# Perceiver cross-attention block: one projection two steps earlier, one PSUM copy on another engine, one exponential ahead of a Gelu

## The chip, the cores and the metric

One core of a Trainium2 chip runs the whole program. Five engines work in parallel, each through its own list of instructions in order, and wait for each other by semaphores: TensorE (matmuls, PE in the profile, its weight loads PEld), VectorE (DVE), ScalarE (ACT), GpSimd (POOL), and SyncE (SP), which here only issues DMAs. The metric is the device time of one execution in microseconds, the median of several.

## The reference, cut to what matters

The block takes `x` (16 batches x 64 rows x 256) and a context (16 batches x 1601 rows x 256) and applies three sublayers with layer norms and residuals. Only the first one, the cross-attention, is touched:

```
Q, K, V = linear(norm(x)), linear(ctx), linear(ctx)      # 16 heads of 16
scores  = Q K^T / 4
feats   = mean(scores), mean of row maxima, variance of softmax(scores)   # per head
hidden  = gelu(linear(gelu(linear(feats))))              # exact gelu, width 64
t       = exp(clip(linear(hidden)))                      # one temperature per head
out     = softmax(Q K^T / (2 t)) V
```

So each batch needs two passes over the scores: a first one for the statistics, from which a small perceptron makes a temperature per head, and a second one with that temperature, whose exponentials are multiplied with V. The second sublayer is a gated state-space mixer, the third a feed-forward net with 4-bit block quantization; in the kernel they are the "tail" of each pair of batches.

## The kernel before, in words

**Slots and steps.** `run` goes through slots, one per batch `b` (from -1 to 19), each of 32 steps (`STEPS`). Every engine has its own `slot` function, which goes through the same 32 steps and issues what belongs to them; since each engine is in order, this written order is the schedule. In slot `b` three things overlap: the first pass of batch `b` (all 32 steps, one unit of scores each: `scores` on TensorE L651, maximum on VectorE L1179, exponential on ScalarE L909, `bn_stats` on VectorE L1185), the second pass of batch `b-1`, and the projections of the context. The tail of each pair of batches is spread over two slots and more.

**First pass.** Unit `u` is a chunk of 400 keys of a pair of heads. TensorE issues scores `u` and `u+1` in even steps. Three PSUM banks and three SBUF rings hold them, so scores `u` wait for exponential `u-3` (`before`). ScalarE runs exponential `u` in step `u+1` (`exp1`), VectorE the sums in step `u+2`.

**Second pass.** Unit `v` (0 to 27, two key tiles of a row group of heads each) has its scores in step `S2_AT[v]`: steps 14 to 37 and 40 to 43, where 32 and more are steps of the next slot; 38 and 39 (steps 6 and 7 of the next slot) are idle. Two units' scores go together (`scores2`, L667 and L677), ScalarE's exponential (`exp2`, L918) comes one step after its unit's, the multiplication with V (`values`, L694) two steps after the scores. So unit 22's exponential stands in step 5 and unit 23's in step 6, and both units' values in step 6. `exp2` writes one of five rings (`pring`), and waits for the multiplication that used the ring before.

**Projections.** `PJ_PLAN` says in which step TensorE projects a tile of 256 context rows into keys (`("k", tile, off)`, L605) or values (`("v", tile, off)`, L612); `off` 0 is this slot's batch, 1 the next one's. All go through one PSUM bank (`pjp`): a projection waits until the last one has been copied away (`pj_free`). ScalarE copies it one step later (`project`, L882 for keys, L869 for values), GpSimd adds up the keys for the mean two steps after the projection (`key_sums`, L1069). The context tile itself must have been split in two parts (`split_context` on ScalarE, L900, and a subtraction on GpSimd, L1083), in the steps of `CTX_AT`; the split of the next tile that uses the same buffer waits for the values' projection.

**Temperature.** `statistics` on VectorE runs in steps 1, 3, 8 and 10. TensorE's three small matmuls (`temperature`, L631, L634, L636) stand in steps 5, 6 and 7; in step 7, which is odd, the small matmul stands behind a projection if there is one. ScalarE's first Gelu is the last thing in step 5, its second the first in step 6 (`gelu`, L888). Gelu and Exp are in different tables, so there is a table load before the first Gelu and one before the exponential that follows. VectorE clips in step 8 (L1230, L1234), ScalarE turns the clipped value into the temperature first thing in step 9 (L985), ahead of that step's `exp2` and `exp1`; VectorE scales Q with it in step 10, and the `("m",)` entry in step 13 (L592) makes the row of shifts that the second pass starts from.

**ScalarE's order in a step** is: second Gelu, temperature, `exp2`, `exp1`, projection's copy, context split, tail, first Gelu. **VectorE's** is: maximum, sums, statistics, key column, tail.

The functions of the diff follow, with the line numbers of the profile.

Of the kernel before, what the change touches and what calls it, by code (L numbers as in the profile page):

```python
# [12 lines left out]
P = 128  # L13
B = 16
SQ = 64
D = 256
DB = D // P
# [18 lines left out]
S2U = VU * PPB  # L36
# [13 lines left out]
STEPS = S1U  # L50
# [8 lines left out]
def unit1(u):  # L59

    return u // NPAIR, S1_P[u]

# [1 line left out]

PJ_PLAN = [(1, ("k", 4, 0)), (3, ("v", 4, 0)), (5, ("k", 5, 0)), (9, ("v", 5, 0)), (11, ("k", 6, 0)),
           (12, ("v", 6, 0)), (13, ("m",)), (17, ("k", 0, 1)), (19, ("v", 0, 1)), (21, ("k", 1, 1)), (23, ("v", 1, 1)),
           (25, ("k", 2, 1)), (27, ("v", 2, 1)), (29, ("k", 3, 1)), (31, ("v", 3, 1))]
N_M = sum(w[0] == "m" for _, w in PJ_PLAN)  # L70
N_OLD = sum(w[0] != "m" and w[-1] == 0 for _, w in PJ_PLAN)
N_NEW = len(PJ_PLAN) - N_M - N_OLD

CTX_AT = {1: (5, 0), 9: (6, 0), 11: (0, 1), 15: (1, 1), 20: (2, 1), 24: (3, 1), 28: (4, 1)}
UNTIL = [(lo + w - 1) // (2 * P) for lo, w in CH]
S2_IDLE = (38, 39)
S2_AT = [s for s in range(14, 14 + S2U + 2) if s not in S2_IDLE]
S1_P = [0, 1, 2, 3, 4, 5, 6, 7, 2, 3, 0, 1, 4, 5, 6, 7] + 2 * list(range(NPAIR))
STATS_AT = [1, 3, 8, 10]
MLP_AT = {5: 0, 6: 1, 7: 2}  # L80
N_MLP = len(MLP_AT)
W_AT, GELU_AT, C_AT = 2, 5, 9
# [51 lines left out]
class Slot:  # L134
# [91 lines left out]
    def plan(self):  # L226

        got = []
        for step, what in PJ_PLAN:
            if what[0] == "m":  # L230
# [10 lines left out]
def need(eng, sem, value):  # L241

    if isinstance(value, int) and value <= 0:
        return
    eng.wait_ge(sem, value)
# [13 lines left out]
def build(nc, t, q_dram, out):  # L259
    ctx = ExitStack()  # L260
    with ctx:
# [39 lines left out]
        kt = [sb(f"kt{i}", [P, DB, SK + 2]) for i in range(2)]  # L301
# [68 lines left out]
        pjp = ps("pjp")  # L370
# [17 lines left out]
        pj_full, pj_free = sem("pj_full"), sem("pj_free")  # L388
# [458 lines left out]
        def _(act):  # L847
# [130 lines left out]
            def slot(s):  # L978
                plan = {step: (use, what) for step, use, what in s.plan()}
                for step in range(STEPS):  # L980
                    if s.has(1, B) and step == GELU_AT + 1:
                        gelu(s, 1)
                    if s.has(1, B) and step == C_AT:
                        need(act, sc, s.lin(SC_N, SC_CLIP - SC_N))
                        nc.scalar.activation(lt[:, 2, :], lt[:, 1, :], ACT.Exp, scale=-1.0).then_inc(c_ready, 1)  # L985
                    s_, v = s.second(step, 1)
                    if s_.has(1, B) and v < S2U:
                        exp2(s_, v)
                    s_, u = s.unit(step, 1)
                    if s_.has(0, B - 1):  # L990
                        exp1(s_, u)
                    if s.has(1, B) and step == W_AT:
                        need(act, sc, s.lin(SC_N, SC_DIFF - SC_N))
                        nc.scalar.activation(st[:, 1, :, :], st[:, 0, :, :], ACT.Exp).then_inc(w_ready, 1)
                    s_, at = s.unit(step, 1)
                    uses = {step_: (use, what) for step_, use, what in s_.plan()}
                    if at in uses:
                        project(s_, *uses[at])
                    if s.b == -1 and step == QUERIES_AT:
                        queries()  # L1000
                    if s.context_at(step):
                        split_context(s, *CTX_AT[step])
                    if s.b in W_SLOT and step - 1 in W_SLOT[s.b]:
                        weights(W_SLOT[s.b][step - 1])
                    if s.last:
                        tail(s.last, step + 2 * STEPS, s)
                    if s.tail:
                        tail(s, step + STEPS * (s.r - 1), s)
                    if s.has(1, B) and step == GELU_AT:
                        gelu(s, 0)  # L1010

# [88 lines left out]
        def _(dve):  # L1100
# [20 lines left out]
            for i, w in enumerate((wk, wv)):  # L1121
                for d in range(DB):
                    hi, lo, raw = wkv[:, i, 0, d, :], wkv[:, i, 1, d, :], w[:, d, :]
# [132 lines left out]
            def key_column(s, what):  # L1256
                need(dve, ks_part, s.lin(VU - 1, (VU - 1) * (what[-1] + 1)))
                nc.vector.tensor_reduce(kt[(s.par + what[-1]) % 2][:, :, SK], ksum[:, :, :], AX.X,
                                        ALU.add).then_inc(ks_ready, 1)

            def finish(s, part):

                if part == 1:
                    return divide(s)
                need(dve, fin_c, s.lin(FIN_N, -2 * FIN_N))
                c = Chain(fin_c, s.lin(FIN_N, -2 * FIN_N))
                pv = pvp[:, 0:2 * P].rearrange("p (g i q) -> p g i q", g=DB, i=2)
                need(dve, pv_done, s.lin(S2U, -S2U))
                c(nc.vector.tensor_scalar(fin[:, 0, :, :], pv[:, :, 1, :], cst[:, 2:3], None, ALU.mult), False)
                c(nc.vector.tensor_scalar(fin[:, 1, :, :], pv[:, :, 0, :], cst[:, 2:3], None, ALU.mult))  # L1270
                c(nc.vector.scalar_tensor_tensor(out=fin[:, 0, :, :], in0=pv[:, :, 0, :], scalar=cst[:, 3:4],
                                                 in1=fin[:, 0, :, :], op0=ALU.mult, op1=ALU.add), False)
                c(nc.vector.scalar_tensor_tensor(out=fin[:, 1, :, :], in0=pv[:, :, 1, :], scalar=cst[:, 3:4],
                                                 in1=fin[:, 1, :, :], op0=ALU.mult, op1=ALU.add))
                assert c.n == FIN_PV
# [113 lines left out]
            def slot(s):  # L1389
                if s.b == -1:  # L1390
                    dve.wait_ge(setup_pe, 8)
                    for i in range(2):
                        nc.vector.memset(vblocks(i)[:, :, HD:2 * HD], 1.0).then_inc(vt_ones, 1)
                for step in range(STEPS):
                    if s.has(0, B - 1):
                        maxima(s, step)
                    s_, u = s.unit(step, 2)
                    if s_.has(0, B - 1):
                        sums(s_, u)
                    if s.has(1, B) and step in STATS_AT:  # L1400
                        statistics(s, STATS_AT.index(step))
                    s_, at = s.unit(step, 4)
                    for at_, use, what in s_.plan():
                        if at_ == at and what[0:2] == ("k", VU - 1):
                            key_column(s_, what)
                    if s.has(2, B + 1) and step in FIN_AT:
                        finish(s, FIN_AT.index(step))
                    if s.b in WQ_SLOT and step in WQ_SLOT[s.b]:
                        weights(WQ_SLOT[s.b][step])
                    if s.last:  # L1410
                        tail(s.last, step + 2 * STEPS, s)
                    if s.tail:
                        tail(s, step + STEPS * (s.r - 1), s)
                if s.b == 2:
                    dve.wait_ge(wt_out, WT_USES)
                    nc.vector.memset(ht[:, :, :, :], 0.0).then_inc(ht_zero, 1)
                    dve.wait_ge(ht_zero, 1)
# [68 lines left out]
```

## Time and profile before

| | us |
|---|---|
| median of 3 runs | 1263.6 |
| lowest and highest of them | 1262.91, 1266.12 |
| the profiled execution | 1263.17 |
| its span in the profile | 1261.0 |
| TensorE busy (matmuls) | 1128.2 |
| VectorE busy | 822.1 |
| ScalarE busy | 769.0 |
| GpSimd busy | 402.9 |

The profile is of one execution. The span runs from its first instruction to its last; the rest of the execution's 1263.17 us lies around it. Busy time is the union of an engine's instructions; a matmul's end is modelled, so two matmuls in flight overlap. The mean TensorE clock granted over the span is 0.874 of 2.4 GHz; it takes two levels, 1.2 and 2.4 GHz. In the chain that ended last TensorE has 70% of the span, VectorE 12%, ScalarE 5%.

### The profile page before, as it was taken

To read this page: it belongs to the slowest core of one execution; us is meant where nothing else is said; L and a number is where in the kernel's file an instruction comes from. 1 tells how busy PE (TensorE), PEld (TensorE's weight loads), DVE (VectorE), ACT (ScalarE), POOL (GpSimd) and SP (SyncE) were. 2 spreads that over 40 slices of the span, in tenths; PEclk is the share of its full clock that TensorE was granted. 3 is DMA by queue.
4 is the path that set the end of the run, shared out by engine and by line. 5 is a ranking of instruction groups with operands and counts; after the bars stand their busy time and mean duration, and the time that the engine had idled before them with its cause. 6 is when DMAs were issued, how large, how long until landed. Compare 5 with 4: busy or idle time off the path is not lost.

```text
span 1261.0 us, 39200 instructions
## 1 busy us (share of the span) xinstructions
PE 1128.2 (89%) x14964; PEld 910.9 (72%) x14964; DVE 822.1 (65%) x2124; ACT 769.0 (61%) x1547; POOL 402.9 (32%) x416
## 2 busy tenths in 40 slices
PE   3778799999999999999899999999999989988935
PEld 3545587878777877878787878787787868766622
DVE  4557667566767777777767776777776876762232
ACT  2434586767657775677577766777666767672310
POOL 2366351313234323333233323432333333201210
PEclk9957798979889997989899988898898989995955
DMA  4601110201010101011110101020101000000000
GB/s 127 194 20 26 30 28 14 57 22 35 4 50 11 52 11 43 19 35 28 26 36 14 49 14 39 11 53 10 43 20 43 19 19 3 6 7 1 3 5 4
DMA packets 46812, 38.85 MB, mean 31 GB/s; under 512 B 14576, under 2 KB 46000, under 8 KB 46640
## 3 DMA queue, kind: packets, MB, share of 16 engines
q1 hardware_dynamic: 46640, 36.41, 10.6%
q8 instruction: 125, 2.05, 0.7%
q14 instruction: 47, 0.39, 0.1%
HBM read 34.30 MB, written 2.10 MB: 29 GB/s over the span
## 4 chain that ended last, share of the span: by engine, by line
PE 70%; DVE 12%; issue 8%; ACT 5%; POOL 2%; DMA 1%; SPq 1%; ACTq 0%; DVEq 0%; POOLq 0%
PE s1p L651 12%; PE s2p L677 12%; PE pjp L612 12%; PE pjp L605 11%; PE pvp L694 8%; DVE est L1185 2%; PE tlp L808 2%; DVE negm L1179 2%; PE tlp L790 2%; PE tlp L784 2%; PE s2p L667 2%; PE tlp L771 1%; ACT pring L918 1%; PE tlp L751 1%; PE tlp L729 1%
## 5 line engine op out<-in xcount | busy, mean ns | idle before, releaser
L1179 DVE TENSOR_REDUCE negm<-s1p 128x1 f32<-128x400 f32 (+1 forms) x512 | 289.3, 565 | 180.5 <-PE s1p L651 175.9
L909 ACT ACTIVATE ering<-s1p,negm 128x400 f32<-128x400 f32 (+1 forms) x512 | 303.4, 597 | 117.8 <-DVE negm L1179 113.0
L918 ACT ACTIVATE pring<-s2p 128x512 f32<-128x512 f32 (+1 forms) x448 | 251.4, 565 | 158.5 <-PE s2p L677 158.0
L1185 DVE BATCH_NORM_STATS2 est<-ering 128x6 f32<-128x400 f32 (+1 forms) x512 | 290.2, 567 | 23.0 <-ACT ering L909 23.0
L651 PE MATMUL s1p<-kt,qbd 32*128 32x400 f32 (+1 forms) x1024 | 292.3, 594 | 12.5 <-ACT ering L909 10.1
L677 PE MATMUL s2p<-q2bd,kt 32*128 32x128 f32 (+1 forms) x3328 | 250.6, 283 | 0.0
L677 PEld LDWEIGHTS s2p<-q2bd,kt 32*128 32x128 f32 (+1 forms) x3328 | 240.1, 193 | 6.9
L605 PE MATMUL pjp<-cr,wkv 128*128 128x256 f32 (+1 forms) x1344 | 203.7, 306 | 26.5 <-DVE vt L1151 18.4
L1083 POOL TENSOR_TENSOR cr<-stage,cr 128x512 fp32r<-128x512 f32 (+1 forms) x112 | 132.0, 1179 | 270.9 <-ACT cr L900 270.9
L605 PEld LDWEIGHTS pjp<-cr,wkv 128*128 128x128 f32 x1344 | 181.6, 208 | 44.8 <-issue 27.6
L612 PE MATMUL pjp<-wkv,cr 128*128 128x256 f32 (+1 forms) x1200 | 193.2, 315 | 9.7 <-ACT kt L882 9.4
L612 PEld LDWEIGHTS pjp<-wkv,cr 128*128 128x128 f32 (+1 forms) x1200 | 168.8, 210 | 35.5 <-ACT kt L882 16.9
L694 PE MATMUL pvp<-pring,vt 128*32 128x64 f32 x6656 | 150.2, 230 | 28.7 <-ACT pring L918 28.6
L694 PEld LDWEIGHTS pvp<-pring,vt 128*32 128x32 f32 x6656 | 109.5, 114 | 68.1 <-ACT pring L918 32.4
L651 PEld LDWEIGHTS s1p<-kt,qbd 32*128 32x128 f32 x1024 | 97.6, 201 | 69.3 <-ACT ering L909 28.9
L1069 POOL TENSOR_TENSOR ksum<-ksum,kt 128x512 f32<-128x512 f32 (+1 forms) x80 | 82.7, 1033 | 182.7 <-ACT kt L882 182.7
L667 PE MATMUL s2p<-shrow,ones_r 32*128 32x512 f32 (+1 forms) x448 | 129.1, 502 | 4.3 <-ACT pring L918 3.2
L882 ACT ACTIVATE kt<-pjp 128x512 f32<-128x512 f32 (+1 forms) x112 | 61.7, 551 | 37.9 <-PE pjp L605 35.9
L1178 DVE COPY feat<-s1p 128x2 f32<-128x2 f32 x128 | 19.7, 154 | 89.8 <-PE s1p L651 89.2
L900 ACT ACTIVATE cr<-stage 128x512 fp32r<-128x512 f32 (+1 forms) x112 | 65.1, 582 | 9.3 <-DMA stage<-in_ctx 9.3
L869 ACT ACTIVATE vt<-pjp 128x512 f32<-128x512 f32 (+1 forms) x108 | 61.1, 566 | 14.8 <-PE pjp L612 10.8
L667 PEld LDWEIGHTS s2p<-shrow,ones_r 32*128 32x128 f32 (+1 forms) x448 | 49.4, 185 | 22.6 <-ACT pring L918 14.6
(186 smaller groups left out, 1005.6 us busy)
## 6 DMA issues: line engine op xcount, KB each, us to landing
stage<-in_ctx SPq DMA_DIRECT2D x96, 256.0 KB, 2.9
qbd<-q_dram SPq DMA_DIRECT2D x128, 8.0 KB, 1.7
stage<-in_ctx SPq DMA_DIRECT2D x16, 65.0 KB, 2.6
vt<-in_x SPq DMA_DIRECT2D x1, 1024.0 KB, 6.8
q_dram<-late SPq DMA_DIRECT2D x1, 1024.0 KB, 4.6
late<-in_x SPq DMA_DIRECT2D x8, 128.0 KB, 2.1
out_y<-late SPq DMA_DIRECT2D x8, 128.0 KB, 1.7
late<-in_gate SPq DMA_DIRECT2D x1, 768.0 KB, 4.9
```

The lines of the kernel that those rows point to most:

```text
L605: mm = nc.tensor.matmul(bank[:, 2 * P * g:2 * P * g + n], wkv[:, 0, wp, d, P * g:P * g + P], c[:, cp, d, 0:n], start=(cp + wp + d == 0), s ...
L612: mm = nc.tensor.matmul(bank[0:m, D * j:D * j + D], c[:, cp, d, P * j:P * j + m], wkv[:, 1, wp, d, :], start=(cp + wp + d == 0), stop=((cp ...
L651: nc.tensor.matmul(s1p[u % 3][:, 0:w], qbd[s.par][rows, g, :], kt[s.par][rows, g, lo:lo + w], start=True, stop=True).then_inc(s1_full, 1)
L667: nc.tensor.matmul(s2p[v % 2][0:ms[0], 0:DB * P * n], ones_r[rows, 0:ms[0]], shrow[rows, :, :].unsqueeze(1).to_broadcast([RT, n, DB, P]), ...
L677: mm = nc.tensor.matmul(s2p[v % 2][0:ms[i], at:at + P], kt[1 - s.par][rows, g, lo:lo + ms[i]], q2bd[1 - s.par][rows, g, :], start=False, s ...
L694: mm = nc.tensor.matmul(pvp[32 * q:32 * q + 32, SQ * r:SQ * r + SQ], vhead(1 - s.par, k + i, ms[i], g, r, j), pring[0:ms[i], v % NPR, at:a ...
L909: nc.scalar.activation(ering[:, u % 3, 0:w], s1p[u % 3][:, 0:w], ACT.Exp, bias=negm[s.par][:, p, c:c + 1]).then_inc(s1_exp, 1)
L918: nc.scalar.activation(pring[0:m, v % NPR, 0:n], s2p[v % 2][0:m, 0:n], ACT.Exp).then_inc(s2_exp, 1)
L1069: nc.gpsimd.tensor_tensor(ksum[:, :, 0:m], was, k[:, :, 2 * P * w:2 * P * w + m], ALU.add).then_inc(ks_part, 1)
L1083: nc.gpsimd.tensor_tensor(c[:, 1, :, 0:n], stage[:, w, :, 0:n], c[:, 0, :, 0:n].bitcast(F32), ALU.subtract).then_inc(ctx_lo, 1)
L1179: nc.vector.tensor_reduce(negm[s.par][:, p, ch:ch + 1], s1p[u % 3][:, 0:w], AX.X, ALU.max, negate=True).then_inc(s1_max, 1)
L1185: nc.vector.bn_stats(est[:, p, ch, :], ering[:, u % 3, 0:CH[ch][1]]).then_inc(s1_sum, 1)
```

## The change

Three edits:

- In `PJ_PLAN` the values' projection of tile 5 moves from step 9 to step 7. ScalarE's copy of it follows one step later as before (step 8 in place of 10). In step 7 it stands ahead of the third small matmul on TensorE.
- The copy of keys' tile 5 (projected in step 5, copied in step 6) is made by VectorE (`key_copy`, behind `statistics` in its step) and no longer by ScalarE.
- The exponential of unit 23 of the second pass (`S2_EARLY`) is no longer in step 6 behind the second Gelu, but in step 5, right before the first Gelu and its table load.

```diff
--- before.py
+++ after.py
@@ -64,7 +64,7 @@
 
 
 
-PJ_PLAN = [(1, ("k", 4, 0)), (3, ("v", 4, 0)), (5, ("k", 5, 0)), (9, ("v", 5, 0)), (11, ("k", 6, 0)),
+PJ_PLAN = [(1, ("k", 4, 0)), (3, ("v", 4, 0)), (5, ("k", 5, 0)), (7, ("v", 5, 0)), (11, ("k", 6, 0)),
            (12, ("v", 6, 0)), (13, ("m",)), (17, ("k", 0, 1)), (19, ("v", 0, 1)), (21, ("k", 1, 1)), (23, ("v", 1, 1)),
            (25, ("k", 2, 1)), (27, ("v", 2, 1)), (29, ("k", 3, 1)), (31, ("v", 3, 1))]
 N_M = sum(w[0] == "m" for _, w in PJ_PLAN)
@@ -75,7 +75,9 @@
 UNTIL = [(lo + w - 1) // (2 * P) for lo, w in CH]
 S2_IDLE = (38, 39)
 S2_AT = [s for s in range(14, 14 + S2U + 2) if s not in S2_IDLE]
+S2_EARLY = S2_AT.index(STEPS + 5)
 S1_P = [0, 1, 2, 3, 4, 5, 6, 7, 2, 3, 0, 1, 4, 5, 6, 7] + 2 * list(range(NPAIR))
+COPY_DVE = ("k", 5, 0)
 STATS_AT = [1, 3, 8, 10]
 MLP_AT = {5: 0, 6: 1, 7: 2}
 N_MLP = len(MLP_AT)
@@ -984,7 +986,7 @@
                         need(act, sc, s.lin(SC_N, SC_CLIP - SC_N))
                         nc.scalar.activation(lt[:, 2, :], lt[:, 1, :], ACT.Exp, scale=-1.0).then_inc(c_ready, 1)
                     s_, v = s.second(step, 1)
-                    if s_.has(1, B) and v < S2U:
+                    if s_.has(1, B) and v < S2U and v != S2_EARLY:
                         exp2(s_, v)
                     s_, u = s.unit(step, 1)
                     if s_.has(0, B - 1):
@@ -994,7 +996,7 @@
                         nc.scalar.activation(st[:, 1, :, :], st[:, 0, :, :], ACT.Exp).then_inc(w_ready, 1)
                     s_, at = s.unit(step, 1)
                     uses = {step_: (use, what) for step_, use, what in s_.plan()}
-                    if at in uses:
+                    if at in uses and uses[at][1] != COPY_DVE:
                         project(s_, *uses[at])
                     if s.b == -1 and step == QUERIES_AT:
                         queries()
@@ -1006,6 +1008,8 @@
                         tail(s.last, step + 2 * STEPS, s)
                     if s.tail:
                         tail(s, step + STEPS * (s.r - 1), s)
+                    if step == GELU_AT and s.prev().has(1, B):
+                        exp2(s.prev(), S2_EARLY)
                     if s.has(1, B) and step == GELU_AT:
                         gelu(s, 0)
 
@@ -1258,6 +1262,13 @@
                 nc.vector.tensor_reduce(kt[(s.par + what[-1]) % 2][:, :, SK], ksum[:, :, :], AX.X,
                                         ALU.add).then_inc(ks_ready, 1)
 
+            def key_copy(s, use, what):
+                _, w, off = what
+                lo = 2 * P * w
+                need(dve, pj_full, use + 1)
+                nc.vector.tensor_copy(kt[(s.par + off) % 2][:, :, lo:lo + 2 * P],
+                                      pjp[:, :].rearrange("p (g k) -> p g k", g=DB)).then_inc(pj_free, 1)
+
             def finish(s, part):
 
                 if part == 1:
@@ -1399,6 +1410,10 @@
                         sums(s_, u)
                     if s.has(1, B) and step in STATS_AT:
                         statistics(s, STATS_AT.index(step))
+                    s_, at = s.unit(step, 1)
+                    for at_, use, what in s_.plan():
+                        if at_ == at and what == COPY_DVE:
+                            key_copy(s_, use, what)
                     s_, at = s.unit(step, 4)
                     for at_, use, what in s_.plan():
                         if at_ == at and what[0:2] == ("k", VU - 1):
```

## Rows read from the trace of the kernel before

**Rows 1.** Page, part 1: busy us (share of the span), instructions.
```profile
PE 1128.2 (89%) x14964; PEld 910.9 (72%) x14964; DVE 822.1 (65%) x2124; ACT 769.0 (61%) x1547; POOL 402.9 (32%) x416
```
**Rows 2.** Waits of TensorE's weight loads: total us, times, longest us.
```profile
PEld pvp L694 <- ACT pring L918: 32.4, 18, 2.1
...
PEld tlp L634 <- ACT hid L888: 10.8, 16, 1.1
PEld tlp L771 <- POOL late L1054: 9.9, 7, 2.6
...
PEld s2p L667 <- ACT shrow L876: 4.2, 11, 0.8
```
**Rows 3.** Timeline, one slot, steps 5 to 10: start us, us, engine, line.
```profile
600.67 1.68 PE L605 MATMUL pjp<-cr,wkv 128*128 128x256 f32 x12
...
602.74 0.94 PE L651 MATMUL s1p<-kt,qbd 32*128 32x400 f32 x4
...
603.71 0.57 DVE L1179 TENSOR_REDUCE negm<-s1p 128x1 f32<-128x400 f32 x1 [0.77 <-PE s1p L651]
...
603.77 0.39 PE L634 MATMUL tlp<-hid,w2s 64*128 64x16 f32 x2
...
605.78 0.60 ACT L918 ACTIVATE pring<-s2p 128x512 f32<-128x512 f32 x1
606.27 0.59 ACT L909 ACTIVATE ering<-s1p,negm 128x400 f32<-128x400 f32 x1
...
606.43 0.65 PE L694 MATMUL pvp<-pring,vt 128*32 128x64 f32 x16 [1.91 <-ACT pring L918]
606.75 0.60 ACT L882 ACTIVATE kt<-pjp 128x512 f32<-128x512 f32 x1
...
607.22 1.09 ACT L909 ACTIVATE ering<-s1p,negm 128x400 f32<-128x400 f32 x2
...
607.55 1.37 PE L651 MATMUL s1p<-kt,qbd 32*128 32x400 f32 x2
...
609.28 0.57 DVE L1179 TENSOR_REDUCE negm<-s1p 128x1 f32<-128x400 f32 x1 [1.81 <-PE s1p L651]
...
609.51 2.80 PE L612 MATMUL pjp<-wkv,cr 128*128 128x256 f32 x12
...
610.71 0.22 ACT L985 ACTIVATE lt<-lt 128x16 f32<-128x16 f32 x1 [2.40 <-DVE lt L1234]
...
611.81 0.37 ACT L918 ACTIVATE pring<-s2p 65x256 f32<-65x256 f32 x1
...
612.24 0.60 PE L651 MATMUL s1p<-kt,qbd 32*128 32x400 f32 x2
```
**Rows 4.** Windows, 12 us from scores 6: PE, PEld, DVE, ACT, POOL busy, PEclk.
```profile
602.80:614.80 12.00, 10.00 (x107) 7.60 (x107) 6.15 (x17) 8.79 (x19) 1.64 (x2) 0.72 0.01 1
672.40:684.40 12.00, 10.09 (x114) 7.54 (x112) 7.15 (x20) 8.41 (x19) 6.32 (x6) 0.86 0.01 3
```
**Rows 5.** Timeline, a slot of the other kind, step 6.
```profile
538.22 0.39 PE L634 MATMUL tlp<-hid,w2s 64*128 64x16 f32 x2
...
538.82 0.57 DVE L1185 BATCH_NORM_STATS2 est<-ering 128x6 f32<-128x400 f32 x1
```
**Rows 6.** Line 1258: ns min/median/max, first and last start.
```profile
L1258 DVE TENSOR_REDUCE kt<-ksum x16: 670/672/690, 79.6 to 1096.8; 128x2 f32<-128x514 f32 x16
```
**Rows 7.** Timeline, a slot with clock 0.86, steps 8 to 10.
```profile
675.89 1.61 PE L651 MATMUL s1p<-kt,qbd 32*128 32x400 f32 x3
...
679.39 0.37 ACT L918 ACTIVATE pring<-s2p 65x256 f32<-65x256 f32 x1
```
**Rows 8.** Timeline, step 12 of the slot of rows 3.
```profile
618.53 1.13 PE L771 MATMUL tlp<-wout,late 128*128 128x256 f32 x4 [0.81 <-POOL late L1054]
```
**Rows 9.** Windows, two slots' steps 12 to 14, columns as in rows 4.
```profile
615.50:621.50 6.00, 5.19 (x54) 3.71 (x55) 4.81 (x13) 2.60 (x6) 3.52 (x6) 1.00 0.17 36
749.00:755.00 6.00, 5.19 (x37) 3.67 (x38) 4.02 (x11) 2.39 (x6) 3.07 (x4) 0.75 0.15 30
```

## What the change does to the time: a prediction

> **What bounds the kernel now.** I read first the busy shares, then the waits of TensorE's weight loads, then the timeline of one batch's slot, then the granted clock over the same steps of all slots. The busy shares show TensorE busy for 1128.2 of 1261.0 us [rows 1]; away from the ends it is the engine that the others follow. The waits show where it stops in the steady part: 32.4 us in 18 stops before the probability-times-values matmuls, on ScalarE's second exponential, and 10.8 us in 16 stops on the first Gelu [rows 2]. Both belong to the same place, steps 5 to 9 of each slot.
>
> The timeline [rows 3] shows the place for one slot. Keys' projection of tile 5 starts at 600.67. TensorE waits a moment for the first Gelu and starts the second small matmul at 603.77. ScalarE runs the second Gelu, loads the Exp table and only then runs unit 23's exponential, at 605.78; TensorE, at unit 23's values matmuls, has waited 1.91 us when they start at 606.43. (Exponentials for the second pass are named by their unit, those of the first pass by exponential and number.) From there it runs without a pause until step 10 (612.24), but slowly: values' projection takes 2.80 us (609.51), where the projection of keys in step 5 took 1.68 us.
>
> The reason stands in the clock rows. Over 12 us from scores 6 on, the mean granted clock is 0.72 or 0.86 [rows 4]; of 15 slots read in this way 12 have 0.71 or 0.72 and 3 have 0.86. At 1.2 GHz in place of 2.4 GHz, 0.72 is (1 - 0.72) x 2 x 12 = 6.7 us of low clock, 0.86 is 3.4 us. The fall comes after the 1.91 us stop, every time.
>
> So the stretch costs two things: the stops, and half speed behind them. But TensorE isn't its only bound: scores 11 need exponential 8 of the first kind, which stands on ScalarE behind the exponential for the temperature (L985), which needs VectorE's clip in step 8, which needs the third small matmul of the perceptron (in VectorE's order the clip also stands behind the maximum of scores 8). That chain runs beside values' projection today: scores 8 start at 607.55, VectorE reads them at 609.28, L985 runs at 610.71, then exponential 8, then unit 25's exponential at 611.81, which ends at 612.18; TensorE is through its projection at 612.3. The two arrive together.
>
> **The change part by part.**
>
> *Second exponential ahead of Gelu.* On ScalarE, consecutive exponentials start 0.49 us apart (605.78 and 606.27 [rows 3]). One goes ahead of the Gelu table load and away from behind the Exp table load. The first Gelu and the two things that wait on it are late by 0.5; exponential 5 of the first kind, which follows the second table load, starts at 606.27 as before. The stop of 1.91 us before unit 23's values is gone: its exponential is through some 2 us before TensorE asks. The stop for the Gelu grows from 0.1 to 0.6 us here (scores 6 and 7 end at 603.68, the second small matmul can start at 604.27). In the other kind of slot, where scores 7 end late anyway (the small matmul at 538.22, behind them [rows 5]), it grows by only 0.1.
>
> *Keys' copy on VectorE.* ScalarE loses 607.22 - 606.75 = 0.47 us from its queue. VectorE gains a copy of 128x512. No such copy is in this trace. Nearest below: 0.57 us for reading 400 columns of PSUM (L1179 [rows 3]); nearest above, 0.67 us for 514 columns [rows 6]. I take 0.65, the 512 columns being next to the latter; 0.5 to 0.9 as bounds, since L1179 writes a single column and a copy writes all. The Trainium skill (VectorE: DVE Perf Modes, The TRN2 errata) gives 120 cycles and one per element for PSUM to SBUF, an estimate of 0.66 us; the sum would be the same. VectorE reaches the copy after its maximum 6 (603.71) and sums 4, that is at about 604.7, and maximum 7 moves from 604.7 to 605.3. That is hidden: exponential 7 doesn't start before 607.26 for ScalarE's own order. What isn't hidden is the new wait: values' projection needs the bank, so TensorE waits for VectorE's copy in step 7, with the third small matmul and scores 8 behind it. GpSimd's key sums of tile 5 only come earlier. No DMA is moved.
>
> *Values' projection in step 7.* After the second small matmul (604.27, 0.32 us) and the values of units 22 and 23 (0.65 us) TensorE is at 605.25; the bank is free at 605.4. At full clock the projection takes 1.6, the third small matmul 0.3: scores 8 start at 607.3, against 607.55 before. In the other kind of slot the copy follows sums 4 (538.82 [rows 5]) and ends at 540.0; scores 8 start at 541.9, against 542.0. From scores 8 on the chain decides. Its length at full clock is in the slot whose clock fell later [rows 7]: scores 8 start at 675.89, unit 25's exponential starts at 679.39 and ends at 679.76, so 3.87 us, against 4.63 (607.55 to 612.18) at low clock. Unit 25's exponential thus ends at 611.2, 1.0 us earlier (0.85 in the other kind), and TensorE has scores 10 behind it by then, worth 0.25: 1.25 and 1.1 us gained at this point. VectorE's third statistics part also moves ahead by 2 us.
>
> But TensorE has nothing between the end of step 8, about 608.8, and scores 11 at 610.8. The projection that covered this is gone. So a new stop of 1.8 to 2.0 us stands in step 10, as long as the one removed. After it I expect the same fall of the clock, but over steps 10 to 13, where TensorE has the most work: with 3.4 us low it costs 1.7 us, with 6.7 us low (of which 0.5 is the stop itself) 3.0 us. The long form arises where the clock falls early in the stop. I take one in four as long: 2.0 us. A little is absorbed (the wait on the shift row in step 14, 4.2 us in 11 stops [rows 2], 0.38 each, since the row is ready earlier): 0.35.
>
> Slots of one kind, six of them, have a further stop in step 12: the projection to the output waits 0.81 us on GpSimd [rows 8], 9.9 us in 7 stops over the whole span [rows 2]. VectorE, being 2 us ahead, hands over earlier, and TensorE arrives later: that stop goes, 0.85 us. In about half of these slots the clock fell behind it (0.75 in one slot's stretch, 1.00 in the other's [rows 9]); that is 3.4 us low, 1.7 us and a little more behind it, over half the slots 1.0.
>
> **The sum.** Six slots: -1.25 + 2.0 - 0.35 - 0.85 - 1.0 = -1.45, together -8.7. Nine others: -1.1 + 2.0 - 0.35 = +0.55, together +5.0. The first slot (no second stage) and the last (no scores, no projections; the Gelu 0.5 later, the Exp 0.5 shorter) I take at 0. The sum is -3.7 us on the profiled execution's 1263.17 (span 1261.0), which is 0.4 under the median: 1259.5, told as 1259. Its own range is 1251 to 1266, since the long or the short low stretch in all slots changes it by 15 x 0.5 up or down.
>
> **The rivals.**
>
> *A: the clock falls in front of the projection.* Before the copy is through, TensorE has stopped twice, 0.6 and 0.15 us in one kind of slot, 0.65 in the other. That stops under 1 us can do it is shown by the output's stop of 0.81 us [rows 8], behind which the clock is 1.00 in that slot and 0.75 in another [rows 9]. The Trainium skill (TensorE: Matmul & The Clock Gate, A second HAM failure mode) says that frequent short idles between groups of matmuls make the clock oscillate; rows 9 agree for one slot of the two. Then the projection takes 2.7 instead of 1.6, scores 8 start at 608.5 and the chain takes 4.6: it ends at 613.1, 0.9 later than before, and the new stop and its low stretch still follow, 1.7 to 2 us. That is some 2.5 us worse than the forecast for such a slot. With four slots in ten it is the point of no gain; with half of them +19 - 4: 1275 or so. Against it: the stops are broken up by matmuls and shorter than the 1.91.
>
> *B: the clock holds behind the new stop, or falls while nothing is lost.* If half the slots pay nothing for it: 7.5 x 2.0 less, 1244. For it: the stop begins later relative to scores 8 if these take long. Against it: all 15 stops of 1.9 us led to a fall.
>
> *C: the gain is hidden.* The output's stop remains, because y's matmul behind the units of step 10 is slowed as well; then -1.85 is missing in six slots: 1270; if only half of it is missing, 1264.
>
> **How the numbers follow.** A measurement of this kernel tells some 0.3%, 3.8 us, from no change. The forecast has 0.42 (0.25 of it under 1259.8, 0.15 within, 0.02 above 1267.4), A 0.24 (slower), B 0.15 (faster), C 0.19 (0.03 faster, 0.12 within, 0.04 slower). So faster 0.43, same 0.27, slower 0.30. The range of 1245 to 1276 reaches to the middle of B and of A.
>
> **What would show it.** Right: no wait of the pvp matmuls on ScalarE in step 6; a Gelu stop longer by 0.5; a VectorE copy of 0.65 us; values' projection at about 1.7 us in step 7; a new stop of 1.8 to 2 us before scores 11 (TensorE on the L909 exponential); the low clock over steps 10 to 13 rather than 6 to 9; fewer stops on L1054. Wrong: projection in step 7 at 2.7 us (A), steps 10 to 13 at clock 1.00 (B), a stop on L1054 as before (C). If scores 11 don't wait, the chain was misread, and the gain is 2 us per slot more.

## The result and the profile after

The changed kernel takes 1315.1 us (median of 4, 1305.3 to 1317.8) against 1264.9 us for the kernel before: a ratio of 1.0377, 95% interval 1.0333 to 1.0421. It is slower by 3.8%; 1259 us were forecast, with 1276 as the far end of the range. Of 19 further runs of the kernel before, taken beside the first four experiments, one took 4597 us at a mean granted clock of 0.193; it is left out of every ratio. The profiled execution has a span of 1312.1 us against 1261.0. The page's busy line, which answers to [rows 1]:

```profile
PE 1171.1 (89%) x14964; PEld 946.0 (72%) x14964; DVE 828.2 (63%) x2140; ACT 762.3 (58%) x1531; POOL 401.6 (31%) x416
```

TensorE has the same 14964 matmuls and is busy 42.9 us longer with them. The mean granted clock is 0.849 in place of 0.874: (1 - 0.849) x 2 x 1312 = 396 us at 1.2 GHz against 318 us. VectorE is busy 6 us longer, ScalarE 7 us shorter; neither explains 51 us. The waits of TensorE's weight loads (total, times, longest), to be read beside [rows 2]:

```profile
PEld s1p L653 <- ACT ering L911: 72.3, 56, 3.7
...
PEld tlp L636 <- ACT hid L890: 16.6, 16, 1.6
...
PEld pjp L614 <- DVE kt L1269: 11.2, 16, 2.4
...
PEld tlp L773 <- POOL late L1058: 4.6, 2, 2.6
```

The 32.4 us before the values matmuls are gone from the list, as meant. In their place the scores wait 72.3 us for an exponential of the first pass. Before, that row was

```profile
PEld s1p L651 <- ACT ering L909: 28.9, 38, 3.7
```

VectorE's copy holds up 11.2 us, the Gelu 5.8 us more. The output's wait on GpSimd fell from 7 stops to 2.

The timeline of one slot of the kind of [rows 3], from keys' projection of tile 5 to scores 14:

```profile
618.22 0.97 PE L607 MATMUL pjp<-cr,wkv 128*128 128x256 f32 x6
...
621.80 0.39 PE L636 MATMUL tlp<-hid,w2s 64*128 64x16 f32 x2 [0.58 <-ACT hid L890]
...
622.13 0.73 PE L696 MATMUL pvp<-pring,vt 128*32 128x64 f32 x32
622.23 0.67 DVE L1269 COPY kt<-pjp 128x512 f32<-128x512 f32 x1
...
622.96 1.68 PE L614 MATMUL pjp<-wkv,cr 128*128 128x256 f32 x12
...
624.89 0.66 PE L653 MATMUL s1p<-kt,qbd 32*128 32x400 f32 x2
...
627.30 0.22 ACT L987 ACTIVATE lt<-lt 128x16 f32<-128x16 f32 x1 [1.43 <-DVE lt L1238]
...
628.36 0.72 PE L653 MATMUL s1p<-kt,qbd 32*128 32x400 f32 x1 [1.96 <-ACT ering L911]
628.40 0.37 ACT L920 ACTIVATE pring<-s2p 65x256 f32<-65x256 f32 x1
...
631.82 2.77 PE L607 MATMUL pjp<-cr,wkv 128*128 128x66 f32 x12
...
634.51 1.70 PE L653 MATMUL s1p<-kt,qbd 32*128 32x400 f32 x4
...
639.91 0.94 PE L653 MATMUL s1p<-kt,qbd 32*128 32x400 f32 x4
```

Up to 628 it is the timeline of the forecast: copy 0.67 us, values' projection at full clock in 1.68, the temperature's exponential at 627.30, and then TensorE before scores 11 with a stop of 1.96 us. From the start of keys' projection to scores 11 it is 10.14 us. The kernel before, in the slot of [rows 3], has scores 11 and 14 here (scores 10 are the row at 612.24):

```profile
612.68 0.50 PE L651 MATMUL s1p<-kt,qbd 32*128 32x400 f32 x2
...
620.04 0.94 PE L651 MATMUL s1p<-kt,qbd 32*128 32x400 f32 x4
```

That is 612.68 - 600.67 = 12.01 us to scores 11: 1.9 us gained. Then comes what was sized wrongly. From scores 11 to scores 14 it is 639.91 - 628.36 = 11.55 us, where it was 620.04 - 612.68 = 7.36. The projection of keys' tile 6 takes 2.77 us, scores 12 and 13 take 1.70, each at half speed. The windows of 4 us, from scores 6 of this slot on (columns as in [rows 4]; the granted clock is third from the end, and (1 - clock) x 2 x the window's length is the time at 1.2 GHz):

```profile
620.30:624.30 4.00, 3.31 (x50) 2.48 (x50) 2.32 (x5) 3.48 (x5) 1.19 (x1) 1.00 0.02 4
624.30:628.30 4.00, 2.10 (x21) 1.29 (x20) 2.98 (x8) 2.57 (x8) 0.00 (x0) 1.00 0.00 0
628.30:632.30 4.00, 3.94 (x35) 3.05 (x35) 3.20 (x12) 3.09 (x9) 0.47 (x1) 0.55 0.02 4
632.30:636.30 4.00, 4.00 (x23) 2.80 (x27) 0.39 (x3) 0.28 (x1) 3.07 (x4) 0.50 0.20 35
636.30:640.30 4.00, 4.00 (x32) 3.38 (x30) 2.57 (x6) 1.74 (x4) 0.00 (x0) 0.67 0.60 164
```

The clock holds through the stop and falls behind it: 0.45 x 2 x 4 + 4 + 0.33 x 2 x 4 = 10.2 us at 1.2 GHz, while TensorE is busy all the time. The slots before had 6.7 or 3.4 us [rows 4]. It is much the same in every slot: all fifteen with a second pass beside them have a stop of 1.93 to 2.03 us before scores 11, and the clock is low behind it for 10.2 us in eleven of them and for longer in the four others.

In one slot of the other kind both the forecast's stop and rival A's are there. Its timeline and its windows:

```profile
696.75 2.76 PE L614 MATMUL pjp<-wkv,cr 128*128 128x256 f32 x12 [0.83 <-DVE kt L1269]
...
703.62 0.89 PE L653 MATMUL s1p<-kt,qbd 32*128 32x400 f32 x1 [2.03 <-ACT ering L911]
```

```profile
696.60:700.60 4.00, 3.85 (x25) 3.59 (x28) 1.15 (x3) 2.51 (x5) 2.75 (x3) 0.57 0.00 0
700.60:704.60 4.00, 1.97 (x21) 1.22 (x15) 3.44 (x10) 1.96 (x6) 0.46 (x1) 0.90 0.00 0
704.60:708.60 4.00, 4.00 (x37) 3.50 (x33) 1.92 (x7) 2.13 (x5) 1.27 (x1) 0.50 0.04 8
708.60:712.60 4.00, 4.00 (x29) 2.37 (x29) 1.30 (x3) 1.47 (x3) 0.44 (x1) 0.50 0.16 25
```

Here TensorE waits 0.83 us for VectorE's copy, the clock falls with the projection (0.57; 2.76 us), is back for a while (0.90), and falls again behind the 2.03 us before scores 11.

### The profile page after: what moved, and what is told of

The parts are those of the page before. It is cut to its first block, busy times and chain, and to the rows that moved or that the text cites. A ratio compares the mean times of both kernels' runs of the same rounds, so it can differ in the third digit from the quotient of the medians.

```text
span 1312.1 us, 39200 instructions
## 1 busy us (share of the span) xinstructions
PE 1171.1 (89%) x14964; PEld 946.0 (72%) x14964; DVE 828.2 (63%) x2140; ACT 762.3 (58%) x1531; POOL 401.6 (31%) x416
## 3 DMA queue, kind: packets, MB, share of 16 engines
q1 hardware_dynamic: 46640, 36.41, 10.2%
## 4 chain that ended last, share of the span: by engine, by line
PE 78%; DVE 11%; issue 4%; ACT 4%; POOL 1%; DMA 1%; SPq 0%; ACTq 0%; DVEq 0%; POOLq 0%
PE pjp L607 14%; PE s1p L653 14%; PE s2p L679 13%; PE pjp L614 13%; PE pvp L696 9%; DVE est L1189 3%; PE s2p L669 2%; PE tlp L792 2%; PE tlp L810 2%; PE tlp L786 2%; DVE negm L1183 2%; PE tlp L731 1%; ACT ering L911 1%; PE tlp L753 1%; PE tlp L773 1%
## 5 line engine op out<-in xcount | busy, mean ns | idle before, releaser
L653 PE MATMUL s1p<-kt,qbd 32*128 32x400 f32 (+1 forms) x1024 | 303.3, 610 | 45.0 <-ACT ering L911 42.6
L679 PE MATMUL s2p<-q2bd,kt 32*128 32x128 f32 (+1 forms) x3328 | 257.6, 286 | 0.0
L679 PEld LDWEIGHTS s2p<-q2bd,kt 32*128 32x128 f32 (+1 forms) x3328 | 244.3, 195 | 7.0
L607 PE MATMUL pjp<-cr,wkv 128*128 128x256 f32 (+1 forms) x1344 | 223.7, 324 | 25.8 <-DVE vt L1155 17.8
L607 PEld LDWEIGHTS pjp<-cr,wkv 128*128 128x128 f32 x1344 | 201.0, 228 | 45.9 <-issue 30.5
L614 PE MATMUL pjp<-wkv,cr 128*128 128x256 f32 (+1 forms) x1200 | 189.6, 311 | 12.9 <-DVE kt L1269 7.6
L614 PEld LDWEIGHTS pjp<-wkv,cr 128*128 128x128 f32 (+1 forms) x1200 | 163.7, 202 | 31.8 <-ACT kt L884 11.7
L653 PEld LDWEIGHTS s1p<-kt,qbd 32*128 32x128 f32 x1024 | 99.3, 206 | 109.4 <-ACT ering L911 72.3
L669 PE MATMUL s2p<-shrow,ones_r 32*128 32x512 f32 (+1 forms) x448 | 135.6, 504 | 5.7 <-ACT pring L920 4.5
L884 ACT ACTIVATE kt<-pjp 128x512 f32<-128x512 f32 x96 | 52.3, 545 | 66.4 <-PE pjp L607 64.5
L669 PEld LDWEIGHTS s2p<-shrow,ones_r 32*128 32x128 f32 (+1 forms) x448 | 52.5, 186 | 24.3 <-ACT pring L920 18.1
```

The costliest lines, as they stand in the source:

```text
L607: mm = nc.tensor.matmul(bank[:, 2 * P * g:2 * P * g + n], wkv[:, 0, wp, d, P * g:P * g + P], c[:, cp, d, 0:n], start=(cp + wp + d == 0), s ...
L614: mm = nc.tensor.matmul(bank[0:m, D * j:D * j + D], c[:, cp, d, P * j:P * j + m], wkv[:, 1, wp, d, :], start=(cp + wp + d == 0), stop=((cp ...
L653: nc.tensor.matmul(s1p[u % 3][:, 0:w], qbd[s.par][rows, g, :], kt[s.par][rows, g, lo:lo + w], start=True, stop=True).then_inc(s1_full, 1)
L669: nc.tensor.matmul(s2p[v % 2][0:ms[0], 0:DB * P * n], ones_r[rows, 0:ms[0]], shrow[rows, :, :].unsqueeze(1).to_broadcast([RT, n, DB, P]), ...
L679: mm = nc.tensor.matmul(s2p[v % 2][0:ms[i], at:at + P], kt[1 - s.par][rows, g, lo:lo + ms[i]], q2bd[1 - s.par][rows, g, :], start=False, s ...
```

## The experiments

Each is compared with runs of the kernel before that were taken beside it. The diffs are against the changed kernel, that of the filler in step 11 against the one with filler in step 9; they are cut. M is the theory that the move uncovers the chain to exponential 8, and that the stop there lowers the clock for the steps behind it; D blames VectorE's copy, G the later Gelu.

**No move.** The two other edits stay.

```diff
-(7, ("v", 5, 0))
+(9, ("v", 5, 0))
```

> The changed kernel with the values' projection of tile 5 back in step 9; the VectorE copy and the early exponential stay. Theory M (the move uncovers the chain to exponential 8, so TensorE stops before scores 11 and does steps 10 to 13 at low clock): no stop before scores 11, steps 10 to 13 at 2.4 GHz, time 1250 to 1268. Rival D (the new wait on VectorE's copy, or the load on VectorE, costs the time): most of the loss stays, over 1295. Rival G (the first Gelu 0.5 us later delays the whole perceptron chain, 15 x 0.5 at least): 1272 to 1280.

Ratio 0.9991 (0.9965 to 1.0017), median 1266.8 us. The loss goes with the move; copy and early exponential together do nothing that can be told from zero. D and G are out as causes of the 3.8%. TensorE doesn't stop before scores 11 in the fifteen slots of its trace that have a second pass beside them, as expected; but the clock isn't at 2.4 GHz throughout behind them: it is low for some of the way from scores 11 to 14 in 12 of the 15 slots, in 7 of them in the kernel before.

**The move alone.**

```diff
-COPY_DVE = ("k", 5, 0)
+COPY_DVE = None
-if s_.has(1, B) and v < S2U and v != S2_EARLY:
+if s_.has(1, B) and v < S2U:
-if step == GELU_AT and s.prev().has(1, B):
-    exp2(s.prev(), S2_EARLY)
```

> The kernel before with the move alone (values' projection of tile 5 in step 7; ScalarE copies keys' tile 5, unit 23's exponential stays behind the second Gelu). Theory M: both stops, the old one of 1.9 us in step 6 and a new one before scores 11, which should be shorter since scores 8 start late; clock low from step 6 to 13; 1300 to 1335. Rival D: without the copy on VectorE the loss is gone, 1260 to 1270.

1.0606 (1.0541 to 1.0671), 1345.6 us, 10 us above the range of M: the direction was right, the size too small. Both stops are in its waits, the new one 1.5 to 2.2 us long; the clock over steps 8 to 13 of one slot (two windows of 8 us) doesn't come up at all:

```profile
PEld s1p L653 <- ACT ering L911: 68.5, 48, 3.7
PEld pvp L696 <- ACT pring L920: 31.3, 16, 2.1
```

```profile
644.00:652.00 8.00, 6.45 (x52) 4.66 (x51) 4.48 (x15) 2.81 (x8) 0.77 (x2) 0.50 0.00 0
652.00:660.00 8.00, 8.00 (x55) 6.20 (x48) 3.48 (x8) 2.88 (x8) 3.07 (x4) 0.50 0.31 71
```

**The temperature's exponential one step later** (changed kernel otherwise), so that exponential 8 doesn't stand behind it on ScalarE.

```diff
-W_AT, GELU_AT, C_AT = 2, 5, 9
+W_AT, GELU_AT, C_AT = 2, 5, 10
```

> The changed kernel with the temperature's exponential (L987) first thing in step 10 in place of step 9 on ScalarE, so that exponential 8 no longer stands behind VectorE's clip. Theory M: the stop of 1.96 us before scores 11 falls to below 0.7, the clock falls in fewer slots, 1235 to 1270. If the stop isn't caused by this chain (rivals D and G): 1305 to 1320.

1.0167 (1.0104 to 1.0230), 1289.9 us: half of the loss is gone, between the two ranges. The chain is the stop's cause. What remains is a stop of 0.6 to 0.8 us (1.3 in one slot), since exponential 8 still follows the maximum of scores 8 and unit 24's exponential:

```profile
612.19 0.60 PE L653 MATMUL s1p<-kt,qbd 32*128 32x400 f32 x1 [0.80 <-ACT ering L911]
```

The clock falls behind this as well, in all fifteen slots and for 6.8 us or more, mostly 10.2. So what this run gains over the changed kernel is the stop's own length, some 1.3 us a slot; what lies behind the stop costs as much as before (the table at the end of this section).

**Filler in step 9.** The changed kernel with twelve more matmuls of the projection's shape where the stop is; their result isn't used.

```diff
+def filler(s, bank):
+    for g in range(2):
+        for k in range(6):
+            nc.tensor.matmul(bank[:, 2 * P * g:2 * P * g + 2 * P], wkv[:, 0, 0, g, 0:P],
+                             wkv[:, 1, 0, g, :], start=(k == 0), stop=(k == 5))
...
+if step == 9 and s.has(0, B - 1):
+    need(pe, pj_free, s.after(("v", 5, 0)))
+    filler(s, pjp)
```

> The changed kernel with 12 more matmuls of the shape of the projection of values in step 9 (on constant weights, into the free projection bank, their result is never read). They add 1.7 us of TensorE work per slot where the stop before scores 11 stands. If it is the low clock behind the stop that costs (half speed in steps 10 to 13, some 5 us per slot): the stop is filled, steps 10 to 13 run at 2.4 GHz, and the kernel is faster than the changed one in spite of the added work, 1245 to 1280. If the stop itself costs and the clock is a side effect: no faster than 1305.

1.0016 (0.9986 to 1.0047), 1271.7 us: 43 us less than the changed kernel, with 192 matmuls more. Timeline and windows of one slot:

```profile
607.68 1.69 PE L622 MATMUL pjp<-wkv 128*128 128x256 f32 x12
...
609.29 1.42 PE L659 MATMUL s1p<-kt,qbd 32*128 32x400 f32 x3
```

```profile
606.40:610.40 4.00, 3.96 (x33) 2.87 (x33) 2.86 (x8) 2.56 (x8) 0.06 (x1) 1.00 0.01 4
610.40:614.40 4.00, 4.00 (x48) 3.03 (x46) 3.46 (x12) 3.15 (x8) 0.80 (x2) 1.00 0.02 4
614.40:618.40 4.00, 4.00 (x31) 3.23 (x30) 2.02 (x5) 1.46 (x3) 2.69 (x4) 0.57 0.18 33
```

The stop is gone, and steps 10 and 11 run at 1.00. Scores 11 start as long after scores 8 as in the changed kernel (3.46 us), since the added matmuls take the stop's place; the gain is all behind them. So the stop's own 2 us aren't what the kernel lost; it lost what came behind it. (A low stretch of 3.4 us still follows in this slot. What set it off I haven't settled.)

**Filler in step 11.** The same twelve matmuls, two steps later, where the clock is low.

```diff
-if step == 9 and s.has(0, B - 1):
-    need(pe, pj_free, s.after(("v", 5, 0)))
+if step == 11 and s.has(0, B - 1):
+    need(pe, pj_free, s.after(("k", 6, 0)))
```

> The changed kernel with the same 12 extra matmuls as in the run with filler in step 9, but in step 11, behind the projection of keys' tile 6: the stop before scores 11 stays open, and the work is added where the clock is low. Theory M says that the 10 us of low clock, not the 2 us of stop, are most of the loss, and that filling the stop prevents them; here they start as before. If the clock stays low through the filler as well (2.9 us per slot of added time): 1345 to 1365. If the denser work brings the clock up sooner, the low stretches are 6.8 us or less in place of 10.2, and the time is 1310 to 1335. Below 1290 theory M is wrong on the stop.

1.0606 (1.0540 to 1.0672), 1339.4 us, between the two ranges. The same work costs 68 us more here than in step 9, 5.9% of the kernel before by the two ratios. Windows of 4 us of one slot, the first with the stop in it:

```profile
631.60:635.60 4.00, 2.12 (x20) 1.39 (x21) 3.20 (x9) 2.65 (x9) 0.12 (x1) 1.00 0.00 0
635.60:639.60 4.00, 4.00 (x38) 3.16 (x35) 3.13 (x12) 2.68 (x7) 0.56 (x2) 0.55 0.05 10
639.60:643.60 4.00, 3.63 (x17) 3.50 (x18) 0.00 (x0) 0.28 (x1) 2.85 (x4) 0.50 0.28 67
643.60:647.60 4.00, 4.00 (x29) 2.48 (x29) 1.38 (x3) 0.59 (x1) 0.00 (x0) 0.50 0.47 124
647.60:651.60 4.00, 4.00 (x28) 3.27 (x28) 2.05 (x7) 1.25 (x3) 0.33 (x2) 0.74 0.01 2
```

The low stretch isn't shorter with the added wide matmuls in it: 13.7 us here (3.6 + 8 + 2.1), and 10.2 or 13.7 us in 13 of the 15 slots. The twelve matmuls themselves take 2.93 us, where they took 1.69 in step 9:

```profile
641.63 2.93 PE L622 MATMUL pjp<-wkv 128*128 128x256 f32 x12 [0.37 <-ACT kt L893]
```

**The early exponential alone**, and **VectorE's copy alone**, each on the kernel before.

```diff
 early exponential alone        VectorE's copy alone
-(7, ("v", 5, 0))              -(7, ("v", 5, 0))
+(9, ("v", 5, 0))              +(9, ("v", 5, 0))
-COPY_DVE = ("k", 5, 0)        -S2_EARLY's two places in ScalarE's slot
+COPY_DVE = None
```

> The kernel before with the early exponential of unit 23 alone. The stop of 1.9 us before unit 23's values goes, but the perceptron's chain is no shorter and exponential 5 starts when it did, so TensorE waits in step 7 or 8 instead (on L911). Theory M: within 0.5% of before, 1258 to 1272. Rival G (the later Gelu costs): 1272 to 1280.

> The kernel before with VectorE's copy of keys' tile 5 alone. Theory M: the copy is hidden, ScalarE is through exponentials 6 and 7 0.47 us earlier, 1258 to 1268. Rival D (VectorE's copy delays the maxima and with them everything): 1272 or more.

The exponential alone gives 0.9955 (0.9926 to 0.9983), 1258.0 us, at the edge of M's range. Its waits, beside the 32.4 and 28.9 us of before:

```profile
PEld s1p L653 <- ACT ering L911: 57.4, 65, 3.7
```

The stop has mostly moved to the scores, which wait for exponential 5; some 6 us remain as gain. The copy alone gives 1.0050 (1.0022 to 1.0078), 1271.7 us: a small loss, where I had it hidden. It lies between the ranges of M and D, and its cause isn't settled.

**Half a projection in each place**, with the later temperature exponential. One key tile of values is projected in step 7, the other in step 9; copy and early exponential stay.

```diff
-(7, ("v", 5, 0))
+(9, ("v", 5, 0))
-W_AT, GELU_AT, C_AT = 2, 5, 9
+W_AT, GELU_AT, C_AT = 2, 5, 10
+if step == 7 and 9 in plan:
+    project(s, *plan[9], (0,))
-    project(s, *plan[step])
+    project(s, *plan[step], (1,) if step == 9 else (0, 1))
...
```

> Both waiting places get real work: half of the values' projection of tile 5 (one key tile, 6 matmuls) in step 7 and the other half in step 9 (ScalarE copies in step 10), with the temperature's exponential in step 10, VectorE's copy and the early exponential as in the changed kernel. Theory M: neither stop exceeds 1 us, the clock holds in most slots, 1225 to 1262. If the clock falls all the same from stops under 1 us: 1262 to 1290.

1258.4 us, the median of ten runs from 1242 to 1277; clearly faster than the changed kernel. That it is faster than the kernel before isn't shown: 0.9906 (0.9864 to 0.9948) is the ratio with its six shortest runs, while the medians of all runs, 1258.4 and 1264.6, are 0.5% apart. In three of the fifteen slots of its trace the clock never falls from scores 6 to 14; here are 16 us of one:

```profile
667.00:671.00 4.00, 3.17 (x50) 2.25 (x50) 2.80 (x6) 3.31 (x7) 3.84 (x3) 1.00 0.01 4
671.00:675.00 4.00, 3.99 (x51) 2.69 (x51) 3.18 (x9) 3.32 (x9) 1.77 (x3) 1.00 0.00 0
675.00:679.00 4.00, 4.00 (x43) 3.17 (x44) 3.34 (x12) 3.13 (x8) 1.71 (x2) 1.00 0.04 8
679.00:683.00 4.00, 4.00 (x35) 3.10 (x34) 3.11 (x9) 2.82 (x9) 0.00 (x0) 1.00 0.19 31
```

The expectation that it holds in most slots wasn't met: it falls in the twelve others, and in five of them it is low for 17.1 us, from about the half projection in step 7 on, though no stop there is over 0.83 us except in the first of these slots. What the split gains over the kernel before lies ahead of scores 11 (the table below); behind them it is still slower.

**The split with the exponential back in step 9.** Only `C_AT` is 9 again.

> The split projection (one half in step 7, one in step 9) with the temperature's exponential back in step 9. Theory M: the chain to exponential 8 is uncovered by half a projection, a stop before scores 11 of 1 to 1.4 us; slower than the split with the later exponential, 1262 to 1300. If the later exponential did nothing there: 1250 to 1262.

1.0183 (1.0114 to 1.0253), 1289.0 us, in the range of M: with half the cover the chain shows again. But it shows otherwise than expected. Where the clock is high, scores 11 start 3.46 us after scores 8 as in the changed kernel (2.3 to 2.7 with the later exponential), while the last stop before them is only 0.24 to 0.65 us in nine slots, not 1 to 1.4; in the six others TensorE has no stop there and is at 1.2 GHz for 17.1 us.

**Filler in step 9 with the later exponential.** `C_AT` is 10 in the kernel with filler in step 9.

> The changed kernel with the filler in step 9 and the temperature's exponential in step 10. The filler covers what the chain leaves in any case, so the later exponential brings nothing or little: 1262 to 1276 (filler with the exponential in step 9: 1271.7). If ScalarE's order counts beyond the stop: under 1255.

0.9886 (0.9831 to 0.9941), 1254.4 us. Not what I expected, but the alternative, that ScalarE's order counts beyond the stop: 1.3 points better than the filler alone, though the filler covers the stop there already. With the exponential in step 9 the filler's end leaves TensorE waiting a little for exponential 8 (1.42 us for three matmuls at 609.29 above, of which the third comes late); that fits the 5.4 us gained from scores 8 to 11 in the table below, but I didn't isolate it.

**The split with filler in step 7**, six matmuls ahead of the half projection.

```diff
+if step == 7 and s.has(2, B - 1):
+    need(pe, s2_exp, s.lin(S2U, S2_EARLY + 1 - 2 * S2U))
+    filler(s, s2p[0])
```

> The split projection with the later exponential, and 6 extra matmuls of 256 columns on constants in step 7 ahead of the half projection, where TensorE stops 0.8 us for VectorE's copy in every second slot. If these stops are what still lowers the clock: the clock holds in more slots, 1225 to 1250. If the added work (0.8 us in each slot, 12 us in all) weighs more: 1258 to 1275.

0.9897 (0.9840 to 0.9955), 1252.7 us, between the two ranges: the same as the split without it within the intervals. The time at 1.2 GHz did fall in its trace (the table), as the expectation had it for the case that the short stops count; from scores 6 to 14 the slots are 14 us shorter together. But the span is only 4 us shorter, so the rest is lost elsewhere in the slots.

**The traces side by side.** The starts of the scores' matmuls (L651, in the later kernels L653 and near) cut each slot into stretches. The table has each run's profiled execution, in us, summed over the fifteen slots from the second on, and the time at 1.2 GHz from scores 6 to 14:

| kernel | scores 6 to 8 | 8 to 11 | 11 to 14 | at 1.2 GHz |
|---|---|---|---|---|
| before | 68 | 81 | 107 | 119 |
| changed | 79 | 54 | 166 | 185 |
| no move | 59 | 79 | 116 | 130 |
| move alone | 113 | 62 | 166 | 251 |
| temperature later | 77 | 35 | 163 | 160 |
| filler in step 9 | 78 | 54 | 120 | 76 |
| filler in step 11 | 75 | 52 | 197 | 182 |
| split, exponential later | 63 | 48 | 134 | 120 |
| split | 64 | 57 | 145 | 144 |
| filler in step 9, exponential later | 79 | 49 | 113 | 71 |
| split, filler in step 7 | 65 | 38 | 127 | 75 |

The changed kernel gains 27 us from scores 8 to 11 and loses 59 from 11 to 14. The later exponential shortens the first of these by 19 us and the second by 3; the filler in step 9 leaves the first as it is and takes 46 us off the second.

## Why the prediction was wrong

- *The bound and the two places where TensorE stops:* right. So was the reading that exponential 8, by way of the clip, stands against values' projection. No move and move alone show that this cover was the whole matter.
- *The early exponential:* right; nothing gained at exponential 5, the Gelu's stop grew by 5.8 us over the span (forecast 0.5 in six slots and 0.1 in nine, 3.9 us).
- *VectorE's copy:* 0.67 us against 0.65. The Trainium skill's figure (VectorE: DVE Perf Modes, The TRN2 errata) was an estimate of 0.66; the trace agrees. The wait for it is 0.83 us in one kind of slot, forecast 0.65. Alone it costs 0.5%, forecast none.
- *Scores 8 and the chain:* scores 8 came 6.67 us after keys' projection (forecast 607.3 - 600.67 = 6.6), unit 25's exponential ended 3.88 us after scores 8 (3.87). The gain to scores 11 was 1.9 us in this slot (1.25); over the fifteen slots it was 26.6 us from scores 8 on, less 10.3 lost ahead of them, 16.3 in all, where the terms -1.25 and -1.1 come to 17.4.
- *The new stop before scores 11:* right, 1.96 and 2.03 us (1.8 to 2.0).
- *The clock behind the stop:* this is the step that failed, the term "2.0" of the sum. I put "1.7 us" for a short low stretch and "3.0 us" for a long one, "one in four as long: 2.0 us". The low stretches measured are 10.2 us or longer. In the slots of the other kind, where no other stop went or came behind scores 11, the way from there to scores 14 grew by 5.1 to 5.3 us in six of nine. Over all fifteen slots it grew by 58.8 us; the forecast for it was 15 x 2.0 less 6 x (0.85 + 1.0), 18.9 us, and the output's stop did go as forecast. Those 40 us are most of the 55 between forecast and result. I had taken the lengths that stand in the kernel before as all that there are. They go with the place in the slot and not with the stop: behind the stop of 0.6 to 0.8 us in the same place (exponential one step later) the stretch is mostly 10.2 us too.
- *"The long form arises where the clock falls early in the stop":* so it looked before. In the slot of [rows 3] the clock is low for 2.0 us of this window, so it fell at 605.2, inside the stop that ended at 606.43; in the slot of [rows 7] it fell 1.0 us behind scores 8, and the stretch was short.

```profile
603.20:607.20 4.00, 2.00 (x39) 1.17 (x36) 1.84 (x4) 3.48 (x7) 0.00 (x0) 0.75 0.02 4
```

In the changed kernel it falls at the end of the stop or up to 0.8 us behind it in fourteen slots, and the stretch is long in all of them. The rule on which the short form was taken for most slots doesn't hold.
- *Rival A* was right as well, on top of the forecast and not in place of it: 0.83 us for the copy, then the projection at 2.76 us. The clock fell there in eight of the fifteen slots, and in four of the five that have a stop of 0.83 us. In each of the eight the way from scores 6 to 8 is 1.0 to 1.7 us longer. I had given both separate chances. The price was also summed wrongly: at 2.5 us a slot, the forecast's gain of 3.7 us is gone with A in 1.5 of 15 slots, not in "four slots in ten", and half of the slots would have made 1278 and not 1275.
- *The parts of the 51 us:* from scores 6 to 14 the six slots of the kind of [rows 3] are longer by 12 us together and the nine others by 30; the other 9 us lie outside these stretches, where the forecast had 5 us of gain from the wait on the shift row.
- *Rival B* (clock holds) didn't occur; all fifteen stops of 2 us were followed by low clock. *C* was wrong: 7 stops on GpSimd became 2.

What stays open: why a stretch behind the new stop lasts 10.2 us and one behind the old 6.7. I suspected the narrow matmuls of steps 10 to 12 (65 and 66 columns or rows); with wide filler among them it still lasted 10.2 or 13.7 us in nearly all slots, so that isn't shown. Open, too, is what the later exponential does by itself in the kernel before, which no run has.

## What to carry to other kernels

Before moving work into a gap, ask what the work covers where it stands: here 1.7 us of projection hid a chain across three engines, and the gap it filled (1.9 us) came back as long, four steps later. Where the clock follows TensorE's stops, price a stop by the work behind it as well as by its own length, and take that price from runs, not from the stretches of the old order. A filler of unused matmuls is a cheap probe for this: if it makes the kernel faster, the clock is the loss. Splitting real work over two gaps did better here than moving it from one to the other (1.0183 against 1.0377), and look at all slots of the trace before saying that the clock holds: the best slot of the split was one of three.

## What the runs showed of the hardware

- The same twelve matmuls made the changed kernel 43 us faster in step 9 (1271.7 against 1315.1) and 24 us slower two steps later (1339.4); in the first place they took 1.69 us at 1.00 clock, in the second 2.93 us at 0.50.
- TensorE can be busy 4.00 of 4.00 us in two windows running and stay at 0.50. Being busy again doesn't by itself bring the clock back within 8 us; the kernel with the move alone had 16 us at 0.50.
- A stop of 2 us was followed by low clock fifteen times out of fifteen in the changed kernel. Stops under 1 us were followed by it in some slots and not in others: of five stops of 0.83 us before values' projection, in four; in the kernel with the filler in step 11, whose slots are the same up to there, the clock fell between scores 6 and 8 in four slots in place of eight. The length of the stop alone doesn't decide it.
- The Trainium skill (TensorE: Matmul & The Clock Gate, A second HAM failure mode) tells of a kernel in which short idles between groups of matmuls make the clock oscillate; the runs agree in some slots and not in others.
